# Small counting steps of a router table: read from SBUF instead of PSUM, and spread one to a scan step

## Chip, cores and metric

The kernel runs on one core of one Trainium2 chip. The metric is the device time of one execution in microseconds (us). The engines are TensorE (PE, with its weight loads as PEld), VectorE (DVE), ScalarE (ACT), GpSimd (POOL) and SyncE (SP), which issues DMAs.

## What is computed

The input `x` has 8 sequences of 1024 tokens of 256 numbers. Two blocks follow each other, each behind a layer norm and with a residual:

```python
x = x + _L0_attn_ref(_layernorm(x, axis=-1), ...)   # a Mamba block: projection, causal conv, selective scan, gate
x = x + _L0_ffn_ref(_layernorm(x, axis=-1), ...)    # a mixture of 8 experts, 2 per token
...
def step(s, inp):                       # selective scan: 512 channels x 16 states, over the tokens
    d_t, B_t, C_t, u_t = inp
    s = jnp.exp(d_t[..., None] * A) * s + d_t[..., None] * B_t[:, None, :] * u_t[..., None]
    return (s, jnp.einsum('bdn,bn->bd', s, C_t))
...
logits = jnp.einsum('bsd,de->bse', x, Wg) + bg
topk_vals, topk_idx = jax.lax.top_k(logits, 2)      # then relu MLP of the two experts, weighted sum
```

## The kernel before

**Scan stage.** The 8192 tokens are cut into `NC` = 16 chunks of 512. A chunk has `SG` = 64 scan steps: 4 groups of 128 channels by 16 states. The vector engine's program is one Python loop, unrolled: `for at in range(STEPS)`, with `c, s = divmod(at, SG)` the chunk and the step in it. Each step does one `scan` (L753, 128x512), after every third state of a group a `weigh` (L765, 128x1024), and then whatever else is due at this step: `add_dt` (L725), `gate` (L775), the statistics of a later chunk (L620 and L629), and the routing steps (`route_step`) of the chunk before. So the order of the work on each engine is written out by hand, and an engine goes through it strictly in that order; engines wait for each other by semaphores. A decay `exp(delta*A)` comes from ACT into PSUM (`ps_a`). The drive, delta*u times B, comes for most states from POOL (`times_b`, L897, 128x1024 from two tiles in SBUF into the ring `dbu`), for four of sixteen states from TensorE. POOL also multiplies a third of the states with C (`weigh` of POOL, L914), makes delta*u (L884), and starts the scatters of routed rows (L871).

**Routing.** A token's two expert assignments get row numbers in a scratch tensor in DRAM, where expert `e` owns a region that begins at `base[e] = e * REG`. `seen` (128x8) holds, for each expert, the next free row. TensorE's "rank" product of chunk `q` puts the new totals into PSUM (`after(q)`), and step 13 of `route_step`, the last one for a chunk, copies them to `seen` (L677). It runs at `s` = 45 of chunk `q + 1`, between two scans.

**The early table.** The expert stage works through tiles of 128 rows. It begins while the last chunk is still being routed, with 57 tiles that the first 8 chunks are sure to have filled (`CUTS = (8, 10, 12, 14, 15)`). For that table and for a later one, `count_tiles` (L682) notes at each cut which tiles of which expert have been begun: `over[:, k] = after(q) > base_row[:, ...]`, with `base_row` made once at the start (L809): `base + tile_row` and the same plus 127. It reads one operand from PSUM and one from SBUF. Two of these six run at chunk 8 (for `q` = 7), the others at chunks 10, 12, 14 and 15, all of them inside step 13. At chunk 9 step 13 also makes a running sum over experts (L669), and eight steps of `early_step` (L685 to L708) turn it into a table of tile places: the first at `s` = 45, the other seven one behind another at `s` = 46. All are 128x8 or 128x1. Each waits for those it reads from by the semaphore `tab_e`. TensorE's rank product for `q` = 9, at `s` = 44 of chunk 10, transposes their result, and step 13 at chunk 10 casts it to integers (L672), which SyncE needs when it loads the first tiles behind chunk 15.

```python
EARLY = {45: (0,), 46: (1, 2, 3, 4, 5, 6, 7)}
...
def count_tiles(q, k, full_or_any):
    dve.tensor_tensor(over[:, k], after(q), base_row[:, full_or_any], ALU.is_gt).then_inc(tab_e, 1)
...
if c == CUTS[0] + 1:
    for j in EARLY.get(s, ()):
        early_step(j)
```

**Expert stage.** Behind the scans, 135 tiles go through two products on TensorE (L2301, L2311), one tile each 3.5 us.

Of the kernel before, what the change touches and what calls it, by code (L numbers as in the profile page):

```python
# [6 lines left out]
P = 128  # L7
# [4 lines left out]
ALU = mybir.AluOpType  # L12
# [7 lines left out]
CUTS = (8, 10, 12, 14, 15)  # L20
# [158 lines left out]
def mamba_block(nc, both, x_t, x1_t, b_dram, ln_g, ln_b, W_in, conv_w, conv_b, W_xproj, W_dt, b_dt, A_log, D_param,  # L179
# [3 lines left out]
    SG = N * G  # L183
# [8 lines left out]
    E = Wg.shape[1]  # L192
# [5 lines left out]
    NK = len(CUTS) + 1  # L198
# [10 lines left out]
    with ExitStack() as ctx:  # L209
        def sb(name, shape, dt=F32):  # L210
            return ctx.enter_context(nc.sbuf_tensor(name, shape, dt))
# [36 lines left out]
        ss = area["ss"].rearrange("p (s h n) -> p s h n", s=2, h=2)  # L248
        over, had, jumped, tile_row, tile_at = both.over, both.had, both.jumped, both.tile_row, both.tile_at
        first_end = sb("early_ends", [P, 1 + E])  # L250
        base_row = sb("base_row", [P, 2, E])
        first_passed, first_jump = (sb(name, [P, E]) for name in ("early_passed", "early_jump"))
        wd = sb("wd", [P, NWD, 2, CH])
        wp = sb("wp", [P, 2, 2, CH])
# [50 lines left out]
        made = sem("masks_made")  # L305
# [49 lines left out]
        DIAGONALS = (54, 57, 61, 63)  # L355
        DRIVE = (4, 4, 10, 10)
        KEEP_EARLY = (4, 9)
        EARLY = {45: (0,), 46: (1, 2, 3, 4, 5, 6, 7)}
        GATE = 3
        TURN_D = {9: 0, 11: 1, 14: 2, 15: 3, 19: 4}  # L360
        TURN_P = {9: 0, 15: 1, 20: 2}
# [105 lines left out]
        def after(q):  # L467
            return proj("rank", 0, q)[:, NT * E:(NT + 1) * E]

        def full_tiles(q):  # L470
            return proj("rank", 0, q)[:, 64:64 + E]
# [12 lines left out]
        def _(sync):  # L484
# [105 lines left out]
            for h in range(2):  # L590
                for m in ((0, 1, 3, 4), (6, 7))[h]:
                    sync.wait_ge(dbu_done, products(t, m))
                    sync.dma_start(*w1_parts[brow(m) + 1]).then_inc(w1_in, 16)
                if h == 0:
                    sync.wait_ge(wd_done, ND * t + 1)
                    sync.wait_ge(wp_done, 3 * t + 1)
                    sync.dma_start(*experts[1]).then_inc(both.w_in, 16)
                    sync.wait_ge(tb_done, 2 * NTP * (t + 1))
                    sync.wait_ge(tab_e, 12)
                    for tile in range(2):  # L600
                        start_tile(sync, both, xs_dram, tile, tile, D)
            sync.wait_ge(exp_done, NC * SG)
# [7 lines left out]
        def _(dve):  # L610
# [21 lines left out]
            def route_step(q, j):  # L632

                if j > 0:
                    dve.wait_ge(*routed(q, {7: 5, 8: 6, 13: 10}.get(j, j - 1)))
                elif q > 0:
                    dve.wait_ge(*routed(q - 1, 13))
                flat = "p i e -> p (i e)"
                wide = [P, NT, E]
                if j == 0:  # L640
                    dve.wait_ge(proj_full, full("logit", 0, q))
                    ins = dve.tensor_reduce(mx[:], logits(q), AX.X, ALU.max)
                elif j == 1:
                    ins = dve.tensor_tensor(equals(q), logits(q), mx[:].unsqueeze(2).broadcast_to(wide), ALU.is_equal)
                elif j in (2, 8):
                    ins = dve.tensor_tensor_scan(cn[:].rearrange(flat), first[:].rearrange(flat),
                                                 equals(q).rearrange(flat), 0.0, ALU.mult, ALU.add)
                elif j in (3, 9):
                    ins = dve.scalar_tensor_tensor(sel[:, j // 9], cn[:], 1.0, equals(q), ALU.is_equal, ALU.mult)
                elif j == 4:  # L650
                    ins = dve.scalar_tensor_tensor(lg[:], sel[:, 0], -3e38, logits(q), ALU.mult, ALU.add)
                elif j == 5:
                    ins = dve.tensor_reduce(second(q), lg[:], AX.X, ALU.max)
                elif j == 6:
                    ins = dve.tensor_tensor(equals(q), lg[:], second(q).unsqueeze(2).broadcast_to(wide), ALU.is_equal)
                elif j == 7:
                    dve.wait_ge(meta, 2 * q)
                    ins = dve.tensor_tensor(ex[:], second(q), mx[:], ALU.subtract)
                elif j == 10:
                    dve.wait_ge(proj_full, full("rank", 0, q))  # L660
                    ins = dve.tensor_tensor(pick[:], sel[:], ranks(q).unsqueeze(1).broadcast_to([P, 2, NT, E]),
                                            ALU.mult)
                elif j == 11:
                    dve.wait_ge(scat, 16 * 2 * NT * q)
                    with nc.allow_low_precision(reason="one term of the sum is not zero, a row number"):
                        ins = dve.tensor_reduce(sli[:], pick[:], AX.X, ALU.add)
                else:
                    if q == CUTS[0]:
                        dve.tensor_tensor_scan(first_end[:, 1:], ones[:, 0:E], full_tiles(q), 0.0, ALU.mult, ALU.add  # L669
                                               ).then_inc(tab_e, 1)  # L670
                    if q == CUTS[0] + 1:
                        dve.tensor_copy(tabi[0:1, :, 0:NE], early_table(q)).then_inc(tab_e, 1)  # L672
                    if q == CUTS[0] - 1:
                        count_tiles(q, 0, 0)
                    if q + 1 in CUTS:
                        count_tiles(q, 1 + CUTS.index(q + 1), 1)
                    ins = dve.tensor_copy(seen[:], after(q))  # L677
                ins.then_inc(routed(q, j)[0], 1)

            def count_tiles(q, k, full_or_any):  # L680

                dve.tensor_tensor(over[:, k], after(q), base_row[:, full_or_any], ALU.is_gt).then_inc(tab_e, 1)  # L682

            def early_step(j):

                if j == 0:
                    dve.wait_ge(tab_e, 3)
                    ins = dve.tensor_scalar(first_end[:, 1:], first_end[:, 1:], float(NE), None, ALU.min)
                elif j == 1:
                    dve.wait_ge(tab_e, 4)  # L690
                    ins = dve.tensor_tensor(had[:, 0], first_end[:, 1:], first_end[:, 0:E], ALU.subtract)
                elif j == 2:
                    ins = dve.tensor_scalar(first_passed[:], first_end[:, 1:], both.lane[:], None, ALU.is_le)
                elif j == 3:
                    dve.wait_ge(tab_e, 5)
                    ins = dve.tensor_scalar(first_jump[:], had[:, 0], float(-P), float(REG), ALU.mult, ALU.add)
                elif j == 4:
                    dve.wait_ge(tab_e, 6)
                    ins = dve.tensor_reduce(tile_at[:, 1:2], first_passed[:], AX.X, ALU.add)
                elif j == 5:  # L700
                    dve.wait_ge(tab_e, 7)
                    ins = dve.tensor_tensor(first_jump[:], first_passed[:], first_jump[:], ALU.mult)
                elif j == 6:
                    dve.wait_ge(tab_e, 9)
                    ins = dve.tensor_reduce(jumped[:], first_jump[:], AX.X, ALU.add)
                else:
                    dve.wait_ge(tab_e, 10)
                    ins = dve.tensor_tensor(tile_at[:, 0:1], jumped[:], tile_row[:], ALU.add)  # L708
                ins.then_inc(tab_e, 1)

            def first_conv(g):
# [91 lines left out]
                ins = dve.tensor_scalar(hx[:, i, :], xb[:, i, :], rr[:, 1, 0, i:i + 1], nb[:, 1, 0, i:i + 1],  # L803
                                        ALU.mult, ALU.add)
            ins.then_inc(norm_done, 1)
            dve.memset(first_end[:, 0:1], 0.0)
            dve.wait_ge(made, 5)
            for k in range(2):
                dve.tensor_scalar(base_row[:, k], base[:], tile_row[:], float((P - 1) * (1 - k)), ALU.add, ALU.add)  # L809
            dve.wait_ge(a_exp, 1)  # L810
            dve.tensor_scalar(a_neg[:], a_neg[:], -1.0, None, ALU.mult).then_inc(const_done, 1)
            for g in range(2):
# [2 lines left out]
            for at in range(STEPS):  # L815
# [16 lines left out]
                for j, offset in enumerate(ROUTE):  # L832
                    q = due(at, offset, -1)
                    if q is not None and q < NC - 1 and j != 12:
                        route_step(q, j)
                if c == CUTS[0] + 1:
                    for j in EARLY.get(s, ()):
                        early_step(j)

        @block.gpsimd  # L840
        def _(pool):
# [509 lines left out]
        def _(pe):  # L1351
# [5 lines left out]
            def project(kind, g, q, part, parts):  # L1357
# [52 lines left out]
                elif kind == "rank":  # L1410
# [3 lines left out]
                    pe.matmul(dst[:, 0:(NT + 1) * E], ident[:], seen[:].unsqueeze(1).broadcast_to([P, NT + 1, E]),  # L1414
                              start=True, stop=False, skip_group_check=True)
                    if q == CUTS[0]:
                        pe.wait_ge(tab_e, 2)
                        pe.matmul(dst[:, 64:64 + E], ones[:], over[:, 0], start=False, stop=False, skip_group_check=True)
                    if q == CUTS[0] + 1:
                        pe.wait_ge(tab_e, 11)  # L1420
                        for k in range(2):
                            pe.matmul(dst[0:1, 64 + k * P:64 + (k + 1) * P], tile_at[:, k:k + 1], ident[:], start=False,
                                      stop=False, skip_group_check=True)
# [183 lines left out]
def moe_block(nc, both, out_bank, x1_t, x1_dram, out_t, xs_dram, w1, w1_in, b1r, b1_in, b2b, gm, bt, small_in,  # L1607
# [5 lines left out]
    NK = len(CUTS) + 1  # L1613
# [41 lines left out]
    with ExitStack() as ctx:  # L1655
        def sb(name, shape, dt=F32):
            return ctx.enter_context(nc.sbuf_tensor(name, shape, dt))
# [176 lines left out]
        def _(dve):  # L1834
# [13 lines left out]
            def tail_step(name):  # L1848
# [56 lines left out]
                elif name == "pad_rows":  # L1905
                    ins = dve.tensor_copy(padi[:], seen[:])
                elif name == "count_last":
                    dve.wait_ge(tab_e, 10 + NK)
                    ins = dve.scalar_tensor_tensor(over[:, NK], seen[:], tile_row[:], base[:], ALU.subtract, ALU.is_gt)
                elif name == "later":  # L1910
                    ins = dve.tensor_copy(later, ps_b[:, 0, 0:NSEG])
# [434 lines left out]
```

## Time and profile before

| | |
|---|---|
| median of 3 runs | 2281.53 us (2281.16 to 2283.25) |
| the profiled execution | 2281.53 us, span of its instructions 2279.7 us |
| busy over the span | PE 92%, DVE 89%, POOL 86%, ACT 74% |
| mean granted TensorE clock | 0.977 |

The span counts from the first to the last instruction. Scans run from 40 us to about 1765 us, the expert stage from there to the end. DVE is busy nearly all of the first and PE nearly all of the second.

### The profile page before, as it was taken

To read this page: it belongs to the slowest core of one execution; us is meant where nothing else is said; L and a number is where in the kernel's file an instruction comes from. 1 tells how busy PE (TensorE), PEld (TensorE's weight loads), DVE (VectorE), ACT (ScalarE), POOL (GpSimd) and SP (SyncE) were. 2 spreads that over 40 slices of the span, in tenths; PEclk is the share of its full clock that TensorE was granted. 3 is DMA by queue.
4 is the path that set the end of the run, shared out by engine and by line. 5 is a ranking of instruction groups with operands and counts; after the bars stand their busy time and mean duration, and the time that the engine had idled before them with its cause. 6 is when DMAs were issued, how large, how long until landed. Compare 5 with 4: busy or idle time off the path is not lost. (4 is left out here: it accounts for less than half of the span.)

```text
span 2279.7 us, 45508 instructions
## 1 busy us (share of the span) xinstructions
PE 2103.7 (92%) x13263; PEld 1713.8 (75%) x13263; DVE 2021.2 (89%) x2844; ACT 1685.4 (74%) x3447; POOL 1969.3 (86%) x1252
## 2 busy tenths in 40 slices
PE   8889899999999998989898989999977999999996
PEld 5667677777777777767677777777767999999885
DVE  5999999999999999999999999999998556657776
ACT  6787879788888888887879788888774544445664
POOL 3988999999999999999999999999997576667775
PEclk9999999999999999999999999999998999999998
DMA  6041414233232415051414142332316677668886
GB/s 192 2 158 46 151 53 153 67 130 102 95 123 74 146 59 175 22 177 38 158 53 144 64 142 72 125 111 85 120 67 212 114 129 156 128 101 162 183 182 153
DMA packets 226007, 263.59 MB, mean 116 GB/s; under 512 B 101123, under 2 KB 182563, under 8 KB 225636
## 3 DMA queue, kind: packets, MB, share of 16 engines
q1 hardware_dynamic: 175172, 208.07, 29.9%
q0 software_dynamic: 29904, 34.77, 8.5%
q10 hardware_dynamic: 20688, 17.85, 2.6%
q8 instruction: 111, 1.82, 0.3%
q14 instruction: 132, 1.08, 0.2%
HBM read 196.75 MB, written 71.71 MB: 118 GB/s over the span
## 5 line engine op out<-in xcount | busy, mean ns | idle before, releaser
L897 POOL TENSOR_TENSOR dbu<-drive_u,w_all 128x1024 f32<-128x1024 f32 x384 | 904.0, 2365 | 45.6 <-DVE ps_a L753 27.6
L1210 ACT ACTIVATE ps_a<-delta,a_neg 128x512 f32<-128x512 f32 x768 | 518.3, 685 | 113.0 <-DVE area L753 98.2
L914 POOL TENSOR_TENSOR wp<-area 128x1024 f32<-128x1024 f32 x192 | 453.1, 2360 | 8.6 <-DVE area L753 8.1
L765 DVE TENSOR_TENSOR wd<-ps_a,area 128x1024 f32<-128x1024 f32 x320 | 383.7, 1199 | 0.0
L1476 PEld LDWEIGHTS ps_y<-ident,wd 128*128 128x128 f32 x2560 | 304.7, 145 | 99.1 <-issue 71.0
L1476 PE MATMUL ps_y<-ident,wd 128*128 128x128 f32 x2560 | 341.6, 279 | 14.5 <-DVE wd L765 14.3
L2059 POOL DMA_INDIRECT acc_scratch<-ow,e_meta x135 | 220.9, 1636 | 132.0 <-DVE ow L1970 120.9
L1503 PEld LDWEIGHTS ps_a<-dg,duT 128*128 128x128 f32 x2048 | 250.8, 198 | 58.5 <-issue 57.3
L1503 PE MATMUL ps_a<-dg,duT 128*128 128x128 f32 x2048 | 260.8, 282 | 30.1 <-ACT carry L1217 27.8
L2301 PEld LDWEIGHTS e_ps_h<-xT,w_tile 128*128 128x128 f32 x2160 | 260.6, 192 | 16.2 <-DVE xT L1948 10.2
L2301 PE MATMUL e_ps_h<-xT,w_tile 128*128 128x128 f32 x2160 | 266.3, 277 | 2.1 <-DVE xT L1948 1.9
L2311 PE MATMUL e_ps_o<-area,e_hT 128*128 x1080 | 255.6, 379 | 0.4 <-DVE e_hT L1955 0.4
L753 DVE TENSOR_TENSOR_SCAN area<-ps_a,carry,dbu 128x512 f32<-128x512 f32 x192 | 242.4, 1262 | 0.0
L753 DVE TENSOR_TENSOR_SCAN ps_a<-ps_a,carry,dbu 128x512 f32<-128x512 f32 x192 | 237.9, 1274 | 0.6 <-issue 0.6
L753 DVE TENSOR_TENSOR_SCAN area<-ps_a,dbu 128x512 f32<-128x512 f32 x192 | 231.0, 1203 | 6.7 <-ACT ps_a L1210 5.0
L753 DVE TENSOR_TENSOR_SCAN ps_a<-ps_a,dbu 128x512 f32<-128x512 f32 x192 | 226.2, 1213 | 4.9 <-ACT ps_a L1210 4.8
L1486 PE MATMUL ps_y<-ident,wp 128*128 128x128 f32 x1536 | 211.6, 283 | 11.3 <-POOL wp L914 11.3
L2108 ACT ACTIVATE e_hT<-e_ps_h,b_turned 128x128 f32<-128x128 f32 x270 | 84.9, 364 | 171.9 <-PE e_ps_h L2301 167.6
L2311 PEld LDWEIGHTS e_ps_o<-area,e_hT 128*128 128x128 f32 x1080 | 194.9, 190 | 21.7 <-issue 0.8
L1486 PEld LDWEIGHTS ps_y<-ident,wp 128*128 128x128 f32 x1536 | 183.2, 147 | 25.0 <-POOL wp L914 16.1
L2100 ACT COPY w_tile<-w_all 128x1024 f32 x135 | 141.0, 1045 | 57.3 <-issue 51.5
L1384 PE MATMUL ps_p<-area 128*128 128x512 f32 x368 | 178.0, 593 | 0.8 <-ACT area L1091 0.8
(247 smaller groups left out, 3825.9 us busy)
## 6 DMA issues: line engine op xcount, KB each, us to landing
area<-b_scratch SPq DMA_DIRECT2D x128, 512.0 KB, 4.9
w_all<-b_scratch SPq DMA_DIRECT2D x96, 512.0 KB, 4.0
dg<-xs_scratch SPq DMA_DIRECT2D x540, 32.0 KB
area<-in_L_attn_x_dram SPq DMA_DIRECT2D x32, 512.0 KB, 5.2
ee<-acc_scratch SPq DMA_DIRECT2D x32, 512.0 KB, 4.1
x_scratch<-area SPq DMA_DIRECT2D x16, 512.0 KB, 2.9
acc_scratch<-area SPq DMA_DIRECT2D x16, 512.0 KB
area<-x_scratch ACTq DMA_DIRECT2D x32, 256.0 KB
```

Source lines behind the costliest of these rows:

```text
L753: dve.tensor_tensor_scan(dst, decay, drive, init, ALU.mult, ALU.add).then_inc(scan_done, 1)
L765: dve.tensor_tensor(wd[:, s % NWD], states(k, 2), cc[:, n:n + 2, :], ALU.mult).then_inc(wd_done, 1)
L897: pool.tensor_tensor(dbu[:, k % NBU], du[:, g % 2, :].unsqueeze(1).broadcast_to([P, 2, CH]), bb[:, row:row + 2, :], ALU.mult).then_inc(dbu ...
L914: pool.tensor_tensor(wp[:, s % 2], ss[:, s % 2], cc[:, rows, :], ALU.mult).then_inc(wp_done, 1)
L1210: act.activation(dst, dl[:, g, :], ACT.Exp, scale=a_neg[:, g, n:n + 1]).then_inc(exp_done, 1)
L1384: ins = pe.matmul(dst, taps[:, g, k, :], xin[:, g, k:k + CH], start=(k == 0), stop=(k == TAPS - 1))
L1476: ins = pe.matmul(ps_y[:, i, :], wd[:, s % NWD, h, i * P:(i + 1) * P], ident[:], start=False, stop=False, is_transpose=True, skip_group_ch ...
L1486: ins = pe.matmul(ps_y[:, i, :], wp[:, s % 2, h, i * P:(i + 1) * P], ident[:], start=False, stop=(j == 2 and h == 1 and i == NT - 1), is_t ...
L1503: ins = pe.matmul(ps_a[:, bank(k), i * P:(i + 1) * P], duT[:, i, :], dg[:, p, h, i, :], start=True, stop=True)
L2059: pool.indirect_dma_start(out=acc_dram, out_offset=bass.IndirectOffsetOnAxis(ap=meta[:, old, 1:].bitcast(U32), axis=0), in_=ow[:, old, :], ...
L2301: ins = pe.matmul(inner(1 - par, j), w1s[:, 1 - par, k, j * P:(j + 1) * P], xT[:, 1 - par, :, k, :], start=(k == 0), stop=(k == KD - 1))
L2311: ins = pe.matmul(ps_o[:, par, 0:D], hT[:, par, k, :], w2[:, bass.ds((e * KF + k) * D, D)], start=(k == 0), stop=(k == KF - 1))
```

## The change

`base_row` is replaced by `base_full`, which is `base + 127` alone and is made late, by a step of its own. The counting no longer reads PSUM inside step 13; it reads `seen` afterwards, as one instruction with three operands in SBUF (`seen - tile_row > base`, with `tile_row` a column). The list `EARLY_AT` names 16 scan steps, and each carries one small instruction: four in chunk 8, eight in a row of steps in chunk 9, one each in chunks 10, 12, 14 and 15. The counts on `tab_e` move accordingly.

```diff
-        base_row = sb("base_row", [P, 2, E])
+        base_full = sb("base_full", [P, E])
...
-        EARLY = {45: (0,), 46: (1, 2, 3, 4, 5, 6, 7)}
+        EARLY_AT = [CUTS[0] * SG + at for at in (47, 48, 50, 51)] + [(CUTS[0] + 1) * SG + at for at in range(46, 54)] + [
+            c * SG + 47 for c in CUTS[1:]]
...
-                    sync.wait_ge(tab_e, 12)
+                    sync.wait_ge(tab_e, 14)
...
                     if q == CUTS[0]:
+                        dve.wait_ge(tab_e, 4)
                         dve.tensor_tensor_scan(first_end[:, 1:], ones[:, 0:E], full_tiles(q), 0.0, ALU.mult, ALU.add
                                                ).then_inc(tab_e, 1)
...
-                    if q == CUTS[0] - 1:
-                        count_tiles(q, 0, 0)
-                    if q + 1 in CUTS:
-                        count_tiles(q, 1 + CUTS.index(q + 1), 1)
                     ins = dve.tensor_copy(seen[:], after(q))
...
-            def count_tiles(q, k, full_or_any):
-
-                dve.tensor_tensor(over[:, k], after(q), base_row[:, full_or_any], ALU.is_gt).then_inc(tab_e, 1)
+            def count_tiles(k, bases):
+                return dve.scalar_tensor_tensor(over[:, k], seen[:], tile_row[:], bases[:], ALU.subtract, ALU.is_gt)
...
                 if j == 0:
-                    dve.wait_ge(tab_e, 3)
+                    dve.wait_ge(*routed(CUTS[0] - 1, 13))
+                    ins = dve.tensor_scalar(base_full[:], base[:], float(P - 1), None, ALU.add)
+                elif j == 1:
+                    ins = dve.memset(first_end[:, 0:1], 0.0)
+                elif j == 2:
+                    dve.wait_ge(tab_e, 1)
+                    ins = count_tiles(0, base_full)
+                elif j == 3:
+                    ins = count_tiles(1, base)
+                elif j == 4:
+                    dve.wait_ge(tab_e, 5)
                     ins = dve.tensor_scalar(first_end[:, 1:], first_end[:, 1:], float(NE), None, ALU.min)
...
-                    dve.wait_ge(tab_e, 10)
-                    ins = dve.tensor_tensor(tile_at[:, 0:1], jumped[:], tile_row[:], ALU.add)
+                    dve.wait_ge(*routed(CUTS[j - 11] - 1, 13))
+                    ins = count_tiles(j - 10, base)
                 ins.then_inc(tab_e, 1)
...
-            dve.memset(first_end[:, 0:1], 0.0)
-            dve.wait_ge(made, 5)
-            for k in range(2):
-                dve.tensor_scalar(base_row[:, k], base[:], tile_row[:], float((P - 1) * (1 - k)), ALU.add, ALU.add)
...
-                if c == CUTS[0] + 1:
-                    for j in EARLY.get(s, ()):
-                        early_step(j)
+                if at in EARLY_AT:
+                    early_step(EARLY_AT.index(at))
...
-                        pe.wait_ge(tab_e, 2)
+                        pe.wait_ge(tab_e, 4)
...
-                        pe.wait_ge(tab_e, 11)
+                        pe.wait_ge(tab_e, 13)
...
-                    dve.wait_ge(tab_e, 10 + NK)
+                    dve.wait_ge(tab_e, 12 + NK)
```

The old `early_step` 0 to 7 keep their operations and become 4 to 11.

## Rows read from the trace of the kernel before

**Rows 1.** Windows, 40 to 1760 us: length, busy PE, PEld, DVE, ACT, POOL.
```profile
40.00:1760.00 1720.00, 1577.99 (x9778) 1236.27 (x9779) 1667.49 (x1792) 1395.21 (x2875) 1610.48 (x928) 0.98 0.32 106
```
**Rows 2.** Waits of DVE and POOL, 200 to 1700 us: total, times, longest.
```profile
DVE delta L725 <- ACT delta L1179: 21.5, 14, 1.8
...
POOL dbu L897 <- DVE ps_a L753: 22.8, 25, 1.2
```
**Rows 3.** Timeline at the start, in front of the scans: start, duration, engine, line.
```profile
34.98 0.69 DVE L725 SCALAR_TENSOR_TENSOR delta<-ps_p,delta 128x512 f32<-128x512 f32 x1 [3.79 <-ACT delta L1179]
```
**Rows 4.** Timeline at chunk 8, step 13: start, duration, engine, line.
```profile
977.50 0.23 DVE L682 TENSOR_TENSOR tile_started<-ps_p,base_row 128x8 f32<-128x8 f32 x2
...
977.64 0.15 DVE L677 COPY seen<-ps_p 128x8 f32<-128x8 f32 x1
...
977.72 1.22 DVE L753 TENSOR_TENSOR_SCAN ps_a<-ps_a,dbu 128x512 f32<-128x512 f32 x1
```
**Rows 5.** Timeline of chunk 9: DVE's scans, the early steps, POOL beside them.
```profile
1079.43 1.26 DVE L753 TENSOR_TENSOR_SCAN ps_a<-dbu,carry,ps_a 128x512 f32<-128x512 f32 x1
...
1080.61 1.26 DVE L753 TENSOR_TENSOR_SCAN area<-ps_a,carry,dbu 128x512 f32<-128x512 f32 x1
...
1084.66 0.17 DVE L688 TENSOR_SCALAR early_ends<-early_ends 128x8 f32<-128x8 f32 x1
...
1084.77 1.29 DVE L753 TENSOR_TENSOR_SCAN ps_a<-ps_a,carry,dbu 128x512 f32<-128x512 f32 x1
...
1085.97 0.15 DVE L691 TENSOR_TENSOR tiles_had<-early_ends 128x8 f32<-128x8 f32 x1
...
1086.14 0.97 POOL L871 DMA_INDIRECT xs_scratch<-area,sli  x1 [0.30 <-issue]
...
1086.78 0.16 DVE L708 TENSOR_TENSOR tile_at<-rows_jumped,tile_row 128x1 f32<-128x1 f32 x1
1086.86 1.28 DVE L753 TENSOR_TENSOR_SCAN area<-ps_a,carry,dbu 128x512 f32<-128x512 f32 x1
```
**Rows 6.** Timeline of chunk 10: one small routing step between two scans.
```profile
1182.15 0.17 DVE L644 TENSOR_TENSOR ps_p<-ps_p,mx 128x32 f32<-128x32 f32 x1
1182.23 1.22 DVE L753 TENSOR_TENSOR_SCAN ps_a<-ps_a,dbu 128x512 f32<-128x512 f32 x1
```
**Rows 7.** Durations of all POOL products L897: min/median/max, first and last start.
```profile
L897 POOL TENSOR_TENSOR dbu<-drive_u,w_all x384: 2337/2363/2422, 37.3 to 1749.6; 128x1024 f32<-128x1024 f32 x192
```
**Rows 8.** DVE groups by form: the old count and the later one from SBUF.
```profile
L682 DVE TENSOR_TENSOR tile_started<-ps_p,base_row 128x8 f32<-128x8 f32 x6 | 0.8, 153 | 0.0
...
L1909 DVE SCALAR_TENSOR_TENSOR tile_started<-seen,tile_row,region_base 128x8 f32<-128x8 f32 x1 | 0.2, 226 | 0.0
```
**Rows 9.** Timeline, chunk 8, s = 50: POOL's product and the scan of s = 51.
```profile
986.17 2.38 POOL L897 TENSOR_TENSOR dbu<-drive_u,w_all 128x1024 f32<-128x1024 f32 x1
986.66 1.20 DVE L753 TENSOR_TENSOR_SCAN area<-ps_a,dbu 128x512 f32<-128x512 f32 x1
```
**Rows 10.** Timeline, chunk 9, s = 48: POOL's product and the scan of s = 49.
```profile
1090.54 2.36 POOL L897 TENSOR_TENSOR dbu<-drive_u,w_all 128x1024 f32<-128x1024 f32 x1
...
1091.94 1.26 DVE L753 TENSOR_TENSOR_SCAN ps_a<-ps_a,carry,dbu 128x512 f32<-128x512 f32 x1
```
**Rows 11.** Timeline, chunk 9, s = 51 to 53: POOL's products and DVE's scans.
```profile
1097.83 2.37 POOL L914 TENSOR_TENSOR wp<-area 128x1024 f32<-128x1024 f32 x1
...
1098.37 2.45 DVE L753 TENSOR_TENSOR_SCAN ps_a<-dbu,carry,ps_a 128x512 f32<-128x512 f32 x2
1100.15 1.28 POOL L884 TENSOR_TENSOR drive_u<-delta,xc 128x512 f32<-128x512 f32 x1
...
1100.73 1.26 DVE L753 TENSOR_TENSOR_SCAN area<-ps_a,carry,dbu 128x512 f32<-128x512 f32 x1
```
**Rows 12.** Timeline, chunk 12, s = 47: POOL's product and the scan of s = 48.
```profile
1410.43 2.36 POOL L914 TENSOR_TENSOR wp<-area 128x1024 f32<-128x1024 f32 x1
...
1412.49 1.22 DVE L753 TENSOR_TENSOR_SCAN area<-ps_a,dbu 128x512 f32<-128x512 f32 x1
```

More of the change, by code:

```diff
@@ L688, in early_step @@
                     ins = dve.tensor_scalar(first_end[:, 1:], first_end[:, 1:], float(NE), None, ALU.min)
-                elif j == 1:
-                    dve.wait_ge(tab_e, 4)
+                elif j == 5:
+                    dve.wait_ge(tab_e, 6)
                     ins = dve.tensor_tensor(had[:, 0], first_end[:, 1:], first_end[:, 0:E], ALU.subtract)
-                elif j == 2:
+                elif j == 6:
                     ins = dve.tensor_scalar(first_passed[:], first_end[:, 1:], both.lane[:], None, ALU.is_le)
-                elif j == 3:
-                    dve.wait_ge(tab_e, 5)
+                elif j == 7:
+                    dve.wait_ge(tab_e, 7)
@@ L696, in early_step @@
                     ins = dve.tensor_scalar(first_jump[:], had[:, 0], float(-P), float(REG), ALU.mult, ALU.add)
-                elif j == 4:
-                    dve.wait_ge(tab_e, 6)
+                elif j == 8:
+                    dve.wait_ge(tab_e, 8)
                     ins = dve.tensor_reduce(tile_at[:, 1:2], first_passed[:], AX.X, ALU.add)
-                elif j == 5:
-                    dve.wait_ge(tab_e, 7)
+                elif j == 9:
+                    dve.wait_ge(tab_e, 9)
                     ins = dve.tensor_tensor(first_jump[:], first_passed[:], first_jump[:], ALU.mult)
-                elif j == 6:
-                    dve.wait_ge(tab_e, 9)
+                elif j == 10:
+                    dve.wait_ge(tab_e, 11)
@@ L705, in early_step @@
                     ins = dve.tensor_reduce(jumped[:], first_jump[:], AX.X, ALU.add)
-                else:
-                    dve.wait_ge(tab_e, 10)
-                    ins = dve.tensor_tensor(tile_at[:, 0:1], jumped[:], tile_row[:], ALU.add)
+                elif j == 11:
+                    dve.wait_ge(tab_e, 12)
+                    ins = dve.tensor_tensor(tile_at[:, 0:1], jumped[:], tile_row[:], ALU.add)
+                else:
+                    dve.wait_ge(*routed(CUTS[j - 11] - 1, 13))
+                    ins = count_tiles(j - 10, base)
```

## Prediction

> **What bounds the kernel now.** I read the windows first: between 40 and 1760 us DVE is busy for 1667.5 of 1720 us and POOL for 1610.5 [rows 1]. The reader is to see that the scan stage is DVE's, and that POOL has little more room. The waits say who leads. In 1500 us of that stage DVE's largest wait is for ACT's delta, 21.5 us in 14 pieces, while POOL's largest is for DVE's scans, 22.8 us [rows 2]. So POOL keeps DVE's pace, and a microsecond that DVE loses between two scans is lost at the end: the expert stage starts when the scans are done. All that the change touches lies on DVE, in and beside the gaps between scans of chunks 8 to 15. The profiled execution took 2281.53 us, which is also the median of the three runs, 1.8 us more than its span; sums are made against 2281.53.
>
> **What is removed.** Three things leave DVE's line of scans. (a) Seven early steps in one gap of chunk 9: from the scan at 1084.77 to that at 1086.86 are 2.09 us, where two scans of the same kind without anything between stand 1.18 us apart, 1079.43 to 1080.61 [rows 5]. The gap costs 0.91 us. (b) The first early step, 1084.66 to the scan at 1084.77: 0.11 us [rows 5]. (c) Six counts inside step 13. The two at chunk 8 begin at 977.50 and the copy behind them at 977.64 [rows 4], so 0.07 us each, 0.42 us. Together 1.44 us. The two instructions that made `base_row` ran before the scans; at the price of the later count, 0.23 us each [rows 8], they are under 0.5 us, and DVE afterwards waits 3.79 us for ACT's delta anyway [rows 3]. They count as nothing; without that cover they would give back 0.5 us.
>
> **What is added, as work.** Sixteen lone small instructions, each in a gap of its own. The trace has such a case: the routing step at 1182.15, with the scan behind it at 1182.23, 0.08 us [rows 6]. The old count took 153 ns; one with three SBUF operands of which one is a column, as it stands later in the same kernel, took 226 ns [rows 8]. I put the 0.07 us between them on top for the six counts and for the comparison with `lane`: 7 x 0.15 = 1.05 us. The other nine (`base_full`, the memset, the minimum, two products, `first_jump`, two sums, `tile_at`) make 9 x 0.08 = 0.72 us. Together 1.77 us, so as pure work the change is +0.33 us. The bounds of this part are not wide: with 0.08 for all it is 1.28 us and the net is -0.16 us; with 0.23 us for each, the whole duration, it is 3.7 us and the net +2.2 us.
>
> **The waits.** TensorE's wait for `tab_e` 4 at chunk 9 comes some 90 us behind the step that gives it, and its wait for 13 in chunk 10 comes as long behind `s` = 53 of chunk 9. SyncE's wait for 14 hangs on the same cast in step 13 of chunk 10 as its wait for 12 did, and what queues behind it are loads at the end of the scans. The new waits of DVE (4 ahead of the running sum, and step 13 ahead of a count) are for its own earlier work. All at 0. TensorE's next product, which waits for the copy to `seen`, gets it 0.07 us earlier at five chunks; TensorE is not the leader there.
>
> **The unknown: what the new instructions run beside.** In the scan stage every DVE instruction that runs beside a POOL product reads at most one tensor from SBUF; the other comes from PSUM, as in the scan (`ps_a` and `dbu`) or the old count [rows 5, 8]. The three early steps that read two SBUF tensors (L691, L702, L708) were run in the one gap in which POOL had only a scatter in hand, 1086.14 to 1087.11 [rows 5]. The change moves them, and makes all six counts of that kind, so nine instructions now read two SBUF tensors at places where POOL is mostly in the middle of a 2.36 us product that reads two as well. No row has this pair. The low end of its price is nothing, as beside the scatter. The high end is that DVE is held until POOL's product ends. POOL's 384 products took between 2337 and 2422 ns [rows 7] whatever DVE did; nothing in the trace shares gradually, so I expect the one end or the other and not a value between.
>
> The high end can be read off place by place, as POOL's end less the start of the scan that follows the gap:
> - count 0 (chunk 8, s = 50): 986.17 + 2.38 - 986.66 = 1.89 us [rows 9]
> - the product of passed and jump (chunk 9, s = 51): 1097.83 + 2.37 - 1098.37 = 1.83 us [rows 11]
> - `tile_at` (s = 53): 1100.15 + 1.28 - 1100.73 = 0.70 us [rows 11]
> - the count of chunk 12 (s = 47): 1410.43 + 2.36 - 1412.49 = 0.30 us [rows 12]; the five others, read likewise, give 0.30 us (chunk 14), 0.10 us (`had`) and nothing (count 1, chunks 10 and 15).
>
> That is 5.12 us. Three of the four `tensor_scalar` steps that go from SBUF to SBUF with one tensor could be held too: the comparison at s = 48, 1090.54 + 2.36 - 1091.94 = 0.96 us [rows 10], `base_full` 0.24 us, and the rest fall on scatters. With them 6.32 us.
>
> I take the high end, 6.32 + 0.33 = +6.65 us, which gives 2288.2 us. It is a narrow choice. For it speaks that the trace keeps the two kinds apart without an exception, so that its cheap prices say nothing about the pair; against it, that all prices it does have are cheap.
>
> The Trainium skill states this case, on the page "SBUF — State Buffer", section "Who interferes with whom": a DVE instruction with two SBUF inputs, or in a two-port mode, and a GpSimd instruction that reads SBUF exclude each other, and the later one blocks until the first has finished. By that rule the addition is the list above; by the rows beside the scatter it is nothing. No row here shows the rule at work.
>
> **Rivals.**
> 1. *The instructions are as cheap beside a product as beside a scatter.* Not slower: +0.33 us, 2281.9 us (2280.5 to 2283.7 by the bounds of the work). For it: 8 elements a row, and the early steps at 0.06 to 0.2 us apart. It decides as soon as the nine together wait less than about 4.2 us.
> 2. *DVE misses its turn.* Where POOL's product ends just ahead of or behind the gap (0 to 0.3 us: `base_full`, `had`, the counts of chunks 10, 12 and 14), POOL's next product may begin first, and DVE is held for 2.36 us more. All five: 11.8 us on top, 2300 us; one or two: 2291 to 2293 us. Against it: POOL's next product often waits for DVE's scan itself [rows 2].
> 3. *Waits are partly absorbed.* The 1.9 us of chunk 8 would shorten DVE's next wait for ACT, 1.5 us on the mean [rows 2]. Then 6.65 - 3 = 3.7 us, 2285 us. Against it: ACT's decays wait for the banks that DVE frees, so ACT is late as well.
> 4. *The burst hid more than its 0.91 us.* POOL's product behind it began only when DVE got on; if such a delay was never made up, 1 to 3 us more come back, 2279 to 2280 us and, with waits at nothing, hardly faster by 0.2%. Against it: POOL waited for DVE there, not DVE for POOL.
>
> **The numbers.** 0.2% is 4.56 us, about what a measurement of this kernel can tell from no change. Held, as forecast or with missed turns: 0.50, its own range 2286 to 2298 us. Held but partly absorbed, within 0.2%: 0.07. Cheap: 0.38. Rival 4 or another gain: 0.03 for over 0.2%, 0.02 below that. So faster 0.03, same 0.47, slower 0.50. The range takes the cheap case from 2280.5 us up and the held one to 2295 us; left out are the upper missed turns and the real gains.
>
> **What would show it.** In the profile after, count 0 behind 985 us: the scan behind it 1.1 us later (cheap) or some 3 us later (held), with POOL's product ended just before the count. The duration of the counts: 0.23 us, or microseconds if the hold is booked in the instruction. The gap of chunk 9 down to 1.2 to 1.3 us from 2.09. If POOL's products next to the counts grow instead, the hold goes the other way and costs POOL, which has little more than 0.1 us to lose each time. The forecast is wrong if the nine show no hold, and too low if holds last longer than the rest of the product.

## The result, and the profile after

The changed kernel is slower: 2299.57 us median (2295.75 to 2304.11, 6 runs) against 2282.39 us (6 runs of the kernel before beside it). The ratio of the runs is 1.0066, 95% interval [1.0055, 1.0077], which is +15.1 us (12.6 to 17.6). The forecast was slower by 6.65 us, 2288.2 us, with a range from 2280.5 to 2295 us. The direction came true, and so did the choice of a hold; the size was more than twice the forecast, and the time lies outside the range.

The page of the kernel after, part 1; DVE's busy time rose by 13.6 us with one instruction fewer, 2843 for 2844, POOL's only by 2.1:

```profile
PE 2116.1 (92%) x13263; PEld 1725.8 (75%) x13263; DVE 2034.8 (88%) x2843; ACT 1685.7 (73%) x3447; POOL 1971.4 (86%) x1252
```

The waits of the kernel after, 200 to 1700 us, against [rows 2]. DVE's wait for ACT is the same; POOL now waits 14 us more for DVE's scans. The second row is taken up below.

```profile
DVE delta L735 <- ACT delta L1184: 21.5, 14, 1.8
DVE ps_a L763 <- PE ps_a L1508: 12.9, 14, 1.6
...
POOL dbu L902 <- DVE ps_a L763: 37.1, 37, 2.4
```

Where the 13.6 us are, the timeline shows. First `base_full`, a `tensor_scalar` of 128x8 that takes 0.17 us when it stands beside a scatter (kernel after, chunk 8, around s = 47; columns start, duration, engine, line):

```profile
984.75 2.37 POOL L919 TENSOR_TENSOR wp<-area 128x1024 f32<-128x1024 f32 x1
985.39 1.39 DVE L621 BATCH_NORM_STATS2 st<-area 128x6 f32<-128x256 f32 x4
986.71 2.76 DVE L685 TENSOR_SCALAR base_full<-region_base 128x8 f32<-128x8 f32 x1
987.08 2.35 POOL L902 TENSOR_TENSOR dbu<-drive_u,w_all 128x1024 f32<-128x1024 f32 x1
989.38 1.21 DVE L763 TENSOR_TENSOR_SCAN area<-ps_a,dbu 128x512 f32<-128x512 f32 x1
```

A hold here means that an instruction lasts until a POOL product beside it ends. POOL's product `wp` ends at 987.12, but the instruction is not let go there: it ends at 989.47, with the *next* product, which ended at 989.43. The hold is booked as duration, so the engine looks busy. The second count of chunk 8 (the prediction had it beside a scatter, at nothing) shows the same with a shorter product behind; it ends at 1000.24, POOL's `drive_u` at 1000.20:

```profile
996.59 2.37 POOL L919 TENSOR_TENSOR wp<-area 128x1024 f32<-128x1024 f32 x1
...
997.86 2.38 DVE L679 SCALAR_TENSOR_TENSOR tile_started<-seen,tile_row,region_base 128x8 f32<-128x8 f32 x1
998.91 1.29 POOL L889 TENSOR_TENSOR drive_u<-delta,xc 128x512 f32<-128x512 f32 x1
```

Chunk 14, s = 47, the longest. 1.74 us of `wp` and all of the next product:

```profile
1643.97 2.38 POOL L919 TENSOR_TENSOR wp<-area 128x1024 f32<-128x1024 f32 x1
1644.62 4.08 DVE L679 SCALAR_TENSOR_TENSOR tile_started<-seen,tile_row,region_base 128x8 f32<-128x8 f32 x1
...
1646.29 2.38 POOL L902 TENSOR_TENSOR dbu<-drive_u,w_all 128x1024 f32<-128x1024 f32 x1
```

In chunk 9 the old burst is gone, 1095.74 to 1096.98 instead of the 2.09 us of [rows 5]. But `first_jump`, one tensor from SBUF to SBUF and a constant, is held to the end of a product at 1107.31:

```profile
1095.74 1.28 DVE L763 TENSOR_TENSOR_SCAN ps_a<-ps_a,carry,dbu 128x512 f32<-128x512 f32 x1
...
1096.93 0.16 DVE L695 TENSOR_SCALAR early_ends<-early_ends 128x8 f32<-128x8 f32 x1
1096.98 1.28 DVE L763 TENSOR_TENSOR_SCAN area<-ps_a,carry,dbu 128x512 f32<-128x512 f32 x1
...
1104.95 2.36 POOL L902 TENSOR_TENSOR dbu<-drive_u,w_all 128x1024 f32<-128x1024 f32 x1 [0.76 <-DVE ps_a L763]
1105.36 1.97 DVE L703 TENSOR_SCALAR early_jump<-tiles_had 128x8 f32<-128x8 f32 x1
```

All held instructions of this execution, each scan behind them against the same scan of the kernel before:

| place | forecast rest | lasted | scans later by |
|---|---|---|---|
| `base_full`, chunk 8 | 0.24 | 2.76 | 2.64 |
| count 0, chunk 8 | 1.89 | 0.85 | 0.77 |
| count 1, chunk 8 | 0 | 2.38 | 2.32 |
| `first_jump`, chunk 9 | 0 | 1.97 | 1.92 |
| count, chunk 12 | 0.30 | 2.75 | 2.64 |
| count, chunk 14 | 0.30 | 4.08 | 2.66 |

Together 12.95 us. Chunk 14 costs less than it lasts, because there the scan had stood idle before for 1.26 us. The other nine and the memset took 0.06 to 0.25 us, although 3.59 of the 6.32 us of the forecast stood with four of them: the product at s = 51, the comparison, `tile_at` and `had`. Less the 0.84 us of the burst, 12.1 us are in these rows, beside a measured difference of 15.1 (12.6 to 17.6).

The profiled execution itself took 2301.22 us, 19.7 more than that of before, and its last scan starts 20.6 us later. Its scans were already 3.1 us behind at the start of chunk 8, ahead of every edit. Of the other 17.5 us, 12.1 are the rows above, 3.9 are three waits for TensorE's drive at s = 42 of chunks 8, 9 and 13 (1.59, 1.14 and 1.16 us), where the profile of before has none, and 1.25 are idle time before the scan at s = 48 of chunk 9. So two single profiles differ by more than the change; the last section says what the waits go with.

### The profile page after: what moved, and what is told of

It reads as the page before. It is cut to its first block and busy times, and to the rows that moved or that the text cites. A ratio compares the mean times of both kernels' runs of the same rounds, so it can differ in the third digit from the quotient of the medians.

```text
span 2299.4 us, 45508 instructions
## 1 busy us (share of the span) xinstructions
PE 2116.1 (92%) x13263; PEld 1725.8 (75%) x13263; DVE 2034.8 (88%) x2843; ACT 1685.7 (73%) x3447; POOL 1971.4 (86%) x1252
## 3 DMA queue, kind: packets, MB, share of 16 engines
q14 instruction: 132, 1.08, 0.2%
## 5 line engine op out<-in xcount | busy, mean ns | idle before, releaser
L1481 PEld LDWEIGHTS ps_y<-ident,wd 128*128 128x128 f32 x2560 | 309.3, 146 | 97.7 <-issue 72.1
L1481 PE MATMUL ps_y<-ident,wd 128*128 128x128 f32 x2560 | 347.1, 282 | 13.0 <-DVE wd L775 13.0
L1508 PE MATMUL ps_a<-dg,duT 128*128 128x128 f32 x2048 | 265.5, 285 | 38.3 <-ACT carry L1222 36.0
```

Source lines behind the costliest of these rows:

```text
L1481: ins = pe.matmul(ps_y[:, i, :], wd[:, s % NWD, h, i * P:(i + 1) * P], ident[:], start=False, stop=False, is_transpose=True, skip_group_ch ...
L1508: ins = pe.matmul(ps_a[:, bank(k), i * P:(i + 1) * P], duT[:, i, :], dg[:, p, h, i, :], start=True, stop=True)
```

## The experiments

Each ratio is against runs of the kernel before on the same chip.

**The spread alone.** The early steps one to a scan step, the counts as they were.

```diff
-        EARLY = {45: (0,), 46: (1, 2, 3, 4, 5, 6, 7)}
+        EARLY = {46 + j: (j,) for j in range(8)}
```

> The kernel before with one edit: the eight early steps stand one to a scan step, s = 46 to 53 of chunk 9; the counts stay in PSUM and in step 13. Theory A (an instruction with two SBUF tensors, or a tensor_scalar from SBUF to SBUF, is held while a POOL product runs, and sometimes through the next product too): in the profile of the changed kernel chunk 9 lost 1.92 us at the fourth early step and won 0.84 us at the old burst, so +1 to +5 us here, with one or two of the eight instructions lasting over 1 us. Rival B (every lone small instruction costs DVE about 1 us, whatever it reads, sixteen of them making the 15 us): +7 us, spread evenly, no long instruction. Rival C (only the counts matter, as instructions that are slow by themselves): -0.3 to 0 us.

Measured: 2285.35 against 2284.3 us, ratio 1.000, [0.9991, 1.001]. In its profile two of the eight were held, `first_passed` for 0.91 and `first_jump` for 1.97 us, against 0.84 us won at the burst. That is net 2 us, which the interval just allows (-2.1 to +2.3 us). Rival B, a price for every lone instruction, would be +7 us and is out. The ratio alone would also fit Rival C, nothing at all; against it stand the two held instructions.

**The counts alone.** `base_full` and the six counts from SBUF at the new places, the burst kept.

```diff
-                    if q == CUTS[0] - 1:
-                        count_tiles(q, 0, 0)
-                    if q + 1 in CUTS:
-                        count_tiles(q, 1 + CUTS.index(q + 1), 1)
...
+        COUNT_AT = [CUTS[0] * SG + at for at in (47, 50, 51)] + [c * SG + 47 for c in CUTS[1:]]
...
+                if at in COUNT_AT:
+                    count_step(COUNT_AT.index(at))
```

> The kernel before with the other part alone: base_full at s = 47 and two counts at s = 50 and 51 of chunk 8, and four counts at s = 47 of chunks 10, 12, 14, 15, all from SBUF; the early steps stay in their burst. Theory A: the holds of the changed profile at these places were 2.64 + 0.77 + 2.32 + 2.64 + 2.66 = 11 us, so +8 to +14 us, ratio 1.0035 to 1.006, with single counts lasting 1 to 4 us. Rival B: +7 us evenly. Together with the other part it should make the whole change, +15 us.

Measured: 1.0043, [1.0031, 1.0055], +9.8 us. The holds are those of the changed kernel within 0.02 us: 2.76, 0.84, 2.39, 2.74 and 4.07 us. The group of counts in its profile (min/median/max):

```profile
L679 DVE SCALAR_TENSOR_TENSOR tile_started<-seen,tile_row,region_base x5: 217/2393/4066, 997.2 to 1750.4; 128x8 f32<-128x8 f32 x5
```

**The whole change beside POOL's scatters.** Same operations and operands, steps at s = 45 and 46.

```diff
-        EARLY_AT = [CUTS[0] * SG + at for at in (47, 48, 50, 51)] + [(CUTS[0] + 1) * SG + at for at in range(46, 54)] + [
-            c * SG + 47 for c in CUTS[1:]]
+        EARLY_AT = {CUTS[0] * SG + 45: (0,), CUTS[0] * SG + 46: (1, 2, 3),
+                    (CUTS[0] + 1) * SG + 45: (4,), (CUTS[0] + 1) * SG + 46: (5, 6, 7, 8, 9, 10, 11)}
+        EARLY_AT.update({c * SG + 46: (11 + k,) for k, c in enumerate(CUTS) if k})
```

> The whole change, with all its operations and operands, but each step placed at s = 45 or 46, where POOL waits for row numbers or runs a scatter: base_full at s = 45 and the memset and both counts at s = 46 of chunk 8, the eight early steps as in the old burst, the later counts at s = 46. Theory A: no product of POOL runs there, so nothing is held: -1 to +1.5 us, ratio 0.9995 to 1.0007, all counts near 0.23 us. If the form of the instructions (three operands in SBUF, a column among them) were slow by itself, or the moved tiles, it stays at +8 to +15 us.

Measured: 1.0002, [0.9991, 1.0014]. The same group, now with nothing to be held by:

```profile
L680 DVE SCALAR_TENSOR_TENSOR tile_started<-seen,tile_row,region_base x5: 202/202/221, 981.0 to 1733.1; 128x8 f32<-128x8 f32 x5
```

So neither the form of the instructions nor the moved tiles cost anything that this can tell, within 2 to 3 us; their place does. For the four later counts the difference is one scan step, s = 46 or s = 47.

**The price by itself.** 64 extra instructions of 128x8, one in each group of 16 states, their result unused, put into the kernel before. Four forms behind the scan n = 1:

```diff
+                if n == 1 and t <= LAST:
+                    dve.wait_ge(scan_done, at + 1)
+                    dve.tensor_tensor(extra[:], base[:], base_row[:, 0], ALU.is_gt)                # two from SBUF
...
+                    dve.tensor_tensor(extra[:], ps_a[:, bank(at), 0:E], base_row[:, 0], ALU.is_gt) # PSUM and SBUF
...
+                    dve.tensor_scalar(extra[:], base[:], 1.0, None, ALU.add)                       # one from SBUF
...
+                    dve.tensor_reduce(extra[:, 0:1], base[:], AX.X, ALU.add)                       # a sum from SBUF
```

> The kernel before plus 64 extra instructions, one in each group of 16 states behind the scan n = 1: a tensor_tensor of 128x8 whose two inputs are in SBUF, its result unused. Theory A: POOL is in a product for about 9 of 10 us, the mean rest of one is 1.2 us and every fifth or so is held for 2.36 us more, so 1.2 to 2 us each, +75 to +130 us, ratio 1.033 to 1.057. Rivals B and C: 0.1 to 0.3 us each for the instruction and its wait for the scan, +6 to +20 us.

> As the run with 64 extra instructions of two SBUF inputs, same places and shape, but one input comes from PSUM (eight columns of the scan's own result). Theory A: never held; 0.1 to 0.3 us each for the instruction and its wait for the scan, +6 to +20 us, ratio under 1.009. If small extra instructions as such were dear: as dear as with two SBUF inputs.

> As before, 64 extra instructions at the same places: a tensor_scalar of 128x8 from SBUF to SBUF with one constant, one tensor input. The changed profile had two such instructions held (base_full 2.76 us, the fourth early step 1.97 us). Theory A in full: held like those with two SBUF inputs, 1.2 to 2 us each, +75 to +130 us. If only a second SBUF input is what counts: +6 to +20 us.

> As before, 64 extra instructions at the same places: a tensor_reduce from 128x8 in SBUF to 128x1 in SBUF, one tensor input. In the changed profile the two early steps of this kind, in front of products, took 0.14 us. Theory A: never held, +6 to +20 us. If any SBUF to SBUF instruction were held: +75 to +130 us.

| form | ratio | interval | us each |
|---|---|---|---|
| two from SBUF | 1.0304 | 1.0288 to 1.032 | 1.08 |
| PSUM and SBUF | 1.0049 | 1.0032 to 1.0067 | 0.17 |
| tensor_scalar, SBUF to SBUF | 1.0339 | 1.0312 to 1.0367 | 1.21 |
| tensor_reduce, SBUF to SBUF | 1.0045 | 1.003 to 1.0061 | 0.16 |

The last column is the excess over before, divided by 64. The extra instruction's group in each profile (count, min/median/max in ns, first and last start), first with two inputs from SBUF:

```profile
L823 DVE TENSOR_TENSOR extra<-region_base,base_row x64: 166/900/4750, 45.3 to 1810.3; 128x8 f32<-128x8 f32 x64
```

With one input from PSUM:

```profile
L823 DVE TENSOR_TENSOR extra<-ps_a,base_row x64: 165/166/167, 45.8 to 1747.4; 128x8 f32<-128x8 f32 x64
```

The `tensor_scalar` from SBUF to SBUF:

```profile
L823 DVE TENSOR_SCALAR extra<-region_base x64: 170/916/5007, 44.1 to 1812.3; 128x8 f32<-128x8 f32 x64
```

The `tensor_reduce` from SBUF to SBUF:

```profile
L823 DVE TENSOR_REDUCE extra<-region_base x64: 160/161/164, 45.5 to 1747.9; 128x1 f32<-128x8 f32 x64
```

The reader is to see that two groups never leave 0.16 us and two spread up to 5. The free ones ran inside a POOL product as well, 52 times of 64. A hold of the plain kind, from the timeline of the form with two SBUF inputs; `wp` ends at 298.18 and the instruction at 298.20:

```profile
295.82 2.36 POOL L918 TENSOR_TENSOR wp<-area 128x1024 f32<-128x1024 f32 x1
296.33 1.21 DVE L754 TENSOR_TENSOR_SCAN ps_a<-ps_a,dbu 128x512 f32<-128x512 f32 x1
297.57 0.63 DVE L823 TENSOR_TENSOR extra<-region_base,base_row 128x8 f32<-128x8 f32 x1
```

The measured 1.08 us is a little under the 1.2 to 2 us expected: 20 of the 64 lasted under 0.3 us, because they met no product or only its last 0.25 us, and the expected fifth that would be held for one product more was a single instruction.

**The turn at a product's end.** The form with two SBUF inputs twice more: behind n = 15 and its weigh, which is the kind of place that s = 47 is, and behind n = 1 without the wait for the scan.

```diff
-                if n == 1 and t <= LAST:
-                    dve.wait_ge(scan_done, at + 1)
+                if n == 15 and t <= LAST:        # the other: n == 1, no wait
```

> 64 extra instructions with two SBUF inputs as in the run with them behind n = 1, but behind the scan n = 15 and its weigh, which is where the changed kernel put base_full and the later counts (s = 47 is such a place), and with no wait of their own. In the changed kernel DVE missed its turn (was held through the next product too) only when the product that ran was wp; behind n = 1 the product was mostly dbu, and it rarely missed. Theory A1 (which product runs, that is the place, decides about a missed turn): most of the 64 find wp running and those with over 0.3 us to go last 2.5 to 4.5 us; +120 to +200 us in all. Theory A2 (missed turns were of those instructions, not of the place): 0.2 to 2.4 us each, the rest of one product, +40 to +90 us.

> As the run with 64 extra instructions of two SBUF inputs behind n = 1, without their wait for the scan. If that wait, which the steps of the changed kernel lack, were what gives DVE its turn at a product's end, holds through the next product appear here and the time rises from 1.030 to over 1.045. If the place decides: the same 1.03 (1.027 to 1.033), less some 5 us for the wait.

Measured: behind n = 15 the ratio is 1.0659, [1.0638, 1.068], 2.35 us each, more than twice the price behind n = 1. Without the wait it is 1.0305, [1.0282, 1.0328], as with it. The group behind n = 15 (busy, mean ns):

```profile
L824 DVE TENSOR_TENSOR extra<-region_base,base_row 128x8 f32<-128x8 f32 x64 | 156.8, 2450 | 0.0
```

Of these 64, 53 began while `wp` ran with a `dbu` product right behind it; 27 of them were held through both (DVE missed its turn), 26 for the rest of the first. Two of them, each with 1.66 us of `wp` left, one let go and one not:

```profile
72.68 2.36 POOL L917 TENSOR_TENSOR wp<-area 128x1024 f32<-128x1024 f32 x1
73.38 1.68 DVE L824 TENSOR_TENSOR extra<-region_base,base_row 128x8 f32<-128x8 f32 x1
...
237.49 2.37 POOL L917 TENSOR_TENSOR wp<-area 128x1024 f32<-128x1024 f32 x1
238.20 4.00 DVE L824 TENSOR_TENSOR extra<-region_base,base_row 128x8 f32<-128x8 f32 x1
239.79 2.37 POOL L900 TENSOR_TENSOR dbu<-drive_u,w_all 128x1024 f32<-128x1024 f32 x1
```

Behind n = 1 the wait makes a difference that the time does not show. With it, 33 instructions began inside a product that had another right behind it, and none missed its turn. Five look like it, because they begin within 0.02 us of the end of `wp`, but the next product had then begun 0.03 to 0.04 us before, and they are held by that one alone (with the wait, n = 1):

```profile
377.98 2.36 POOL L901 TENSOR_TENSOR dbu<-drive_u,w_all 128x1024 f32<-128x1024 f32 x1
378.01 2.36 DVE L823 TENSOR_TENSOR extra<-region_base,base_row 128x8 f32<-128x8 f32 x1
```

Without the wait, 13 of 39 such instructions missed their turn, seven of them with a `dbu` product running. So it is not `wp` alone that makes DVE miss it, as A1 had it, and the instruction's own wait, or the later start that it brings, counts too. In both runs one instruction more was held through two products that began only behind its own start, here without the wait:

```profile
1810.44 0.98 POOL L874 DMA_INDIRECT xs_scratch<-area,sli  x1 [4.05 <-PE ps_y L1489]
1811.00 5.14 DVE L822 TENSOR_TENSOR extra<-region_base,base_row 128x8 f32<-128x8 f32 x1
1811.44 2.35 POOL L917 TENSOR_TENSOR wp<-area 128x1024 f32<-128x1024 f32 x1
```

It began during a scatter, 0.44 us ahead of `wp`, where 0.16 us would have been enough; the other one (4.75 us) and one of the `tensor_scalar` form (5.01 us) began at the same place. So a scatter beside the instruction was free in these runs everywhere but there. The place sets the mean price, 2.35 against 1.08 us; what decides for one instruction between one product and two stays open.

**The counts moved in the changed kernel, and the changed kernel again**, on one chip.

```diff
+        EARLY_AT = {CUTS[0] * SG + 45: (0,), CUTS[0] * SG + 46: (1, 2, 3)}
+        EARLY_AT.update({(CUTS[0] + 1) * SG + 46 + j: (4 + j,) for j in range(8)})
+        EARLY_AT.update({c * SG + 46: (11 + k,) for k, c in enumerate(CUTS) if k})
```

> The changed kernel with the counts alone moved back one scan step: base_full at s = 45, the memset and two counts at s = 46 of chunk 8, the later counts at s = 46 of chunks 10, 12, 14, 15, where POOL waits for row numbers or scatters. The eight early steps stay spread over s = 46 to 53 of chunk 9. The holds of the counts were 11 us in the changed profile and those of the early steps about 2. Hold theory: most of the loss is gone, 0 to +4 us against the kernel before, like the run with the spread alone (ratio 0.999 to 1.002). If the rest of the 15 us is not in single instructions but in the whole arrangement, it stays above +6 us.

> The changed kernel once more, unaltered, on the same chip as its repair. The two halves measured 1.0000 and 1.0043 of the kernel before, the whole 1.0066 in another session. If the halves add up, this comes at 1.004 to 1.006 (+9 to +14 us); if they make each other worse, at 1.0065 or more.

Measured: 1.0058, [1.0041, 1.0075], for the changed kernel, and 1.0022, [1.0012, 1.0033], with the counts moved. Most of the loss goes with the counts. The changed kernel is again what its halves make, +13.2 us (9.4 to 17.1) beside 9.8 and 0, within their intervals. What is left with the counts moved is 5.0 us (2.7 to 7.5), a microsecond above the expectation, where the spread alone had measured nothing. The two profiles show the same two holds; this one's:

```profile
1090.07 0.94 DVE L701 TENSOR_SCALAR early_passed<-early_ends,lane 128x8 f32<-128x8 f32 x1
...
1092.70 1.98 DVE L704 TENSOR_SCALAR early_jump<-tiles_had 128x8 f32<-128x8 f32 x1
```

Less the 0.84 us of the burst they explain 2 us of the 5. In the same profile waits for TensorE's drive at s = 42 of chunks 10 and 12 (1.58 and 1.60 us) and 1.72 us idle before the scan at s = 48 of chunk 10 come on top, but the spread alone, at a ratio of 1.000, has such waits in its profile as well (1.56, 1.18 and 1.59 us, and 1.70 idle). So they can't be put down to the change, and the remaining 3 us stay open. No arrangement tried beats the kernel before; the best of them, beside the scatters, equals it.

## Why the prediction was half right

*What bounds the kernel:* right. DVE's lost time arrives at the end: 64 extra instructions added 156.8 us of busy time in the profile behind n = 15 and about 151 us to the measured time.

*Removed and added work, +0.33 us:* right within what can be told. The change beside the scatters, which keeps the burst and has all the added instructions with nothing held, measures 1.0002, -2.1 to +3.2 us. The gap of chunk 9 shrank by 0.84 us, where 0.91 less 0.08 was worked out. The two instructions at the start and the waits on `tab_e` cost nothing visible.

*Held or free, nothing between:* right, and the narrow choice for "held" was the right one; of the two-product holds that came beside, more below. Rival 1 (free, 0.38) fell with the pair of two SBUF inputs, 1.0304, and one from PSUM, 1.0049. The rule of the Trainium skill ("SBUF — State Buffer", section "Who interferes with whom") agrees with the measurement in all four forms: two SBUF inputs held, a `tensor_scalar` from SBUF to SBUF held, a PSUM operand free, a `tensor_reduce` free. It says that the later instruction blocks until the first finishes; the 2.76 and 4.08 us show that this can be two products long.

*The forms:* partly. `base_full` and `first_jump` were rightly among the suspects, and `first_passed`, forecast at 0.96 us, lasted 0.20 us in one profile and 0.91 to 0.94 in three others.

*The step that failed is the list of rests*, "the high end is that DVE is held until POOL's product ends", 5.12 us and with the `tensor_scalar` steps 6.32. The holds came to 12.95. Two things were wrong with it. The first is the size: at the four places where the product was followed by another without a gap and at least 0.4 us of it was left, DVE was held through the next one too, 2.76, 2.38, 2.75 and 4.08 us. This was Rival 2. It was priced as an addition, 2291 to 2293 us for one or two places and 2300 us for all five near misses, and the upper of these was left out of the range; the evidence against it, that POOL's next product often waits for DVE, did not hold at these four. Three of its five places missed their turn and a fourth place, count 1, did so unforeseen; that its 2300 us lie next to the measured 2299.57 is luck. The second is the reading place by place. It took positions from a trace without holds. Behind the first hold of 2.64 us POOL stands otherwise against DVE, and count 1, read beside a scatter, met `wp`, while count 0 and the product at s = 51 (1.83 us forecast, 0.23 measured) got off lightly. Only 2.73 of the 6.32 us stood at places that were then held. The new positions are not chance from one execution to the next: the profiles of the counts alone and of the changed kernel again have the same five holds of the counts and `base_full` within 0.02 us. They could not be read from a trace in which nothing was held.

*Absorption, Rival 3:* only at chunk 14, where 1.26 us of idle time took part of 4.08. The wait for ACT stayed at 21.5 us in 14 pieces. *Rival 4* (1 to 3 us more come back) finds nothing in the profiles: in the four with the steps spread the gap of the burst gave back 0.84 to 0.85 us, and no scan of chunk 9 behind it gained more than 0.01. The ratio of the spread alone, 1.000 with holds of net 2 us, would not have ruled it out.

## What to carry to other kernels

In this kernel, where VectorE and GpSimd are both nearly full, a VectorE instruction of 8 elements a row cost 1 to 2.4 us on the mean and up to 5 if it read two tensors from SBUF, or went from SBUF to SBUF as a `tensor_scalar`; with one operand in PSUM, or in a gap in which GpSimd ran only a scatter, it cost 0.1 to 0.2, with one place as the exception. When a price depends on what runs beside it, take the mean over positions and not the positions of a trace that the price itself will shift, and let the range hold the whole of the next instruction as well. Such a hold appears as a long duration of a tiny instruction and not as a wait: compare the largest time in a group with its smallest.

## What the runs showed beside this

The kernel's executions scatter by several microseconds, 2278.9 to 2290.0 us in one session, and part of it goes with TensorE's clock (over these 23 executions time and granted clock correlate at -0.64). In the kernel before, the stretches around step 42 of chunk 8 and of chunk 14 differ by their granted clock (columns: length, busy PE, PEld, DVE, ACT, POOL, clock, DMA share, GB/s):

```profile
960.00:975.00 15.00, 15.00 (x113) 12.57 (x111) 14.34 (x23) 13.01 (x26) 13.23 (x8) 1.00 0.24 77
1605.00:1620.00 15.00, 15.00 (x97) 12.04 (x96) 12.89 (x21) 11.40 (x23) 12.27 (x8) 0.89 0.08 28
```

Its timeline on PE shows the same two groups in both, at 2.4 GHz in the first and for a while at half of it in the second:

```profile
966.11 1.04 PE L1486 MATMUL ps_y<-ident,wp 128*128 128x128 f32 x8
966.99 3.60 PE L1390 MATMUL ps_p<-xc,area 128*96 128x512 f32 x8
...
1609.92 1.91 PE L1486 MATMUL ps_y<-ident,wp 128*128 128x128 f32 x8
1611.63 4.36 PE L1390 MATMUL ps_p<-xc,area 128*96 128x512 f32 x8
```

DVE's scan at s = 42 of chunk 14 then waited 1.59 us for TensorE's drive:

```profile
1616.92 2.34 DVE L753 TENSOR_TENSOR_SCAN ps_a<-dbu,ps_a 128x512 f32<-128x512 f32 x2 [1.59 <-PE ps_a L1503]
```

Such waits of over 1 us came at s = 42 in 3 chunks of that execution and in 7 of the changed kernel's; in the waits above, the row PE ps_a is 12.9 us, where the kernel before has 7.4. In seven profiles (the two kernels, the changed one again, and the four runs that move steps or leave a part out) chunks 1 to 14 have 39 such waits at s = 42, 1.14 to 1.60 us, each with a stretch at half clock that began 5 to 7 us before, and 59 scans that did not wait, none with such a stretch. The mean granted clock was 0.977 before, 0.971 after, and 0.947 with the extra instructions behind n = 15. The more DVE is held, the lower the clock; whether a hold brings it down, or both only occur together, no run here separates, and it may be where the missing microseconds of the 15 are, and of the 5 with the counts moved (median granted clock 0.975, against 0.978 beside it).
